# Cross-attention and a routed FFN: copies moved from VectorE to ScalarE and GpSimd, paddings written earlier, equal weight rows copied on the chip

## What is computed

```python
# x, ctx: (64, 128, 512) float32; mask: (64, 128)
x = x + xattn(layernorm(x), ctx, mask)      # softmax(x ctx^T / sqrt(512)) ctx, one head, per batch entry
x = x + ffn(layernorm(x))                   # 8192 tokens, 8 experts, top 2 of 8

scores = softmax(h @ G)                     # G: (512, 8); h is the normalised token
w = top-2 of scores, zero elsewhere
out = sum_e w_e * (silu(h gate_e^T) * (h up_e^T)) down_e^T     # expert width 64
out = out + sum_e w_e * (h A_e^T) B_e^T                        # rank 16
```

## Time and profile before

| | before |
| --- | --- |
| median of 3 runs | 509.11 us (508.49 to 510.6) |
| the profiled execution | 508.56 us, its span 506.8 us |
| busy, share of the span | PE 97%, PEld 86%, DVE 92%, ACT 68%, POOL 57% |
| bytes | HBM read 114.04 MB, written 78.73 MB; 373 GB/s by the DMA engines |
| granted PE clock | 0.99 in the mean, 1.00 during the sweep |

### The profile page before, as it was taken

The page is one execution under the profiler, slowest core; times in us unless marked ns, Lnnn a source line. Parts: engine busy times, 40 slices in busy tenths (PEclk is TensorE's granted clock), DMA queues, the critical chain, the costliest instruction groups (busy, mean ns, idle before and its releaser), DMA issues.

```text
span 506.8 us, 16153 instructions
## 1 busy us (share of the span) xinstructions
PE 489.3 (97%) x4040; PEld 434.1 (86%) x4040; DVE 464.8 (92%) x1855; ACT 343.3 (68%) x927; POOL 290.4 (57%) x411
## 2 busy tenths in 40 slices
PE   7999999999999999899999999999999999999994
PEld 7888888888888887789888999988999999999992
DVE  5899999999999998789989999998999999999995
ACT  4777888878877788778767887876444444444441
POOL 4227677667777568866775445444445445445444
PEclk9999999999999999999999999999999999999997
DMA  8999999999999999999999999969999999999941
GB/s 303 400 317 343 405 408 405 404 397 408 406 408 402 404 327 308 381 383 412 412 413 412 409 403 375 364 243 327 418 414 415 415 417 416 416 414 415 370 170 69
DMA packets 65607, 189.10 MB, mean 373 GB/s; under 512 B 9582, under 2 KB 9710, under 8 KB 65520
## 3 DMA queue, kind: packets, MB, share of 16 engines
q1 hardware_dynamic: 44352, 120.20, 62.2%
q0 software_dynamic: 20800, 67.65, 33.5%
q10 hardware_dynamic: 368, 0.22, 0.1%
HBM read 114.04 MB, written 78.73 MB: 380 GB/s over the span
## 4 chain that ended last, share of the span: by engine, by line
PE 48%; DVE 5%; POOL 5%; issue 5%; ACT 1%; POOLq 0%; ACTq 0%; DVEq 0%
PE rd L519 11%; PE bank L519 11%; PE bank L497 10%; PE rd L535 6%; PE rd L536 5%; PE rd L526 3%; POOL z_rows L1252 2%; DVE z_own L1140 1%; DVE z_shared L1140 1%; DVE ggT_b L1130 1%; POOL x_rows L1240 1%; PE bank L370 1%; DVE ggT_a L1129 1%; DVE xe L797 1%; DVE t L1113 1%
## 5 line engine op out<-in xcount | busy, mean ns | idle before, releaser
L674 ACT COPY hT<-bank 128x512 f32<-128x512 f32 x140 | 82.0, 586 | 50.6 <-PE bank L497 49.8
L1240 POOL DMA_INDIRECT x_rows<-xe x64 | 64.5, 1008 | 43.9 <-DVE xe L797 26.4
L519 PE MATMUL bank<-wg_sb,hT 128*128 x560 | 80.3, 286 | 0.4 <-ACT hT L674 0.4
L519 PE MATMUL rd<-wg_sb,hT 128*128 x560 | 80.2, 286 | 0.0
L370 PE MATMUL bank<-cc_sb,xnT 128*128 128x136 f32 x512 | 80.1, 286 | 0.0
L519 PEld LDWEIGHTS bank<-wg_sb,hT 128*128 128x128 f32 x560 | 72.6, 190 | 0.6 <-issue 0.6
L519 PEld LDWEIGHTS rd<-wg_sb,hT 128*128 128x128 f32 x560 | 72.6, 190 | 0.1
L370 PEld LDWEIGHTS bank<-cc_sb,xnT 128*128 128x128 f32 x512 | 68.4, 191 | 0.3
L535 PE MATMUL rd<-dn_a,ggT_a 128*128 x140 | 67.1, 480 | 1.4 <-DVE ggT_b L1130 1.3
L1255 POOL DMA_INDIRECT out_x<-z_shared x41 | 39.9, 973 | 42.8 <-DVE z_shared L1140 38.7
L1140 DVE SCALAR_TENSOR_TENSOR z_shared<-rd,z_shared 128x512 f32<-128x512 f32 x77 | 57.7, 749 | 2.1 <-PE rd L536 0.4
(11 more groups left out here) (185 smaller groups left out, 1183.1 us busy)
## 6 DMA issues: line engine op xcount, KB each, us to landing
cc_sb<-in_cc SPq DMA_DIRECT2D x64, 532.0 KB, 7.3
z_shared<-z_rows SPq DMA_DIRECT2D x41, 516.0 KB, 20.2
x_sb<-in_x SPq DMA_DIRECT2D x64, 256.0 KB, 6.4
z_own<-z_rows SPq DMA_DIRECT2D x29, 516.0 KB, 19.0
z_shared<-x_rows SPq DMA_DIRECT2D x36, 260.0 KB, 12.0
z_own<-x_rows SPq DMA_DIRECT2D x34, 260.0 KB, 11.1
z_rows<-pad SPq DMA_DIRECT2D x8, 516.0 KB, 7.6
wg_sb<-in_wg SPq DMA_DIRECT2D x8, 288.0 KB, 6.0
```

The source lines that it names most:

```text
L519: mm = pe.matmul(gu_ps[q % 2][:, 0:GU], hT[:, q % 2, k, :], wg_flat[:, bass.ds(at + k * GU, GU)], start=(k == 0), stop=(k == KD - 1))
L674: act.copy(hT[:, q % 2, :, :], hT_ps[q % 2][:].rearrange("p (k s) -> p k s", k=KD)).then_inc(hT_ready, 1)
L1240: pool.indirect_dma_start(out=x1_rows[:, :], out_offset=rows_at(row, ROW1), in_=row, in_offset=None, bounds_check=ROWS - 1, oob_is_err=Fal ...
```

## The change

DVE's `keep_part` becomes an ACT copy with a scale, called between `keep_pT` and `keep_prod`; DVE's `mask_scores` waits for it. `number` moves from DVE (after the fourth tile's sum of weights) to POOL, behind the scatter of the same step. The eight paddings of `x1_rows` go from tiles 10, 16, ... 52 to tiles 6, 7, 8, 8, 9, 9, 10 and 11. Of an odd down piece only the rows from `KG` are loaded (64 KB); its high part is taken of these rows alone, `dn_hi` is zero in the others (a memset on POOL), and instead of `down_left` ACT copies the equal rows of the even piece, as POOL has left them.

```diff
+PADDED_AT = [6, 7, 8, 8, 9, 9, 10, 11]
...
+        def down_rows(i):
+            return slice(0, P) if i % 2 == 0 else slice(KG, P)
...
-                if n % 6 == 4 and (n - 10) // 6 in range(E):
-                    at = (PADS + [NOWHERE])[(n - 10) // 6]
-                    if n == 10:
-                        sp.wait_ge(pad_set, 2)
-                    sp.dma_start(x1_rows[at:at + P, :], pad[:, D:ZW]).then_inc(padded[0], 16)
+                for i in range(E):
+                    if n == PADDED_AT[i]:
+                        at = (PADS + [NOWHERE])[i]
+                        if i == 0:
+                            sp.wait_ge(pad_set, 2)
+                        sp.dma_start(x1_rows[at:at + P, :], pad[:, D:ZW]).then_inc(padded[0], 16)
                 if n + 6 in SUMS_AT:
                     i = SUMS_AT.index(n + 6)
-                    sp.dma_start(dn_part(i).bitcast(F32), dn[:, i % 2, i // 2, :]).then_inc(dn_loaded, 16)
+                    if i % 2 == 0:
+                        sp.dma_start(dn_part(i).bitcast(F32), dn[:, i // 2, :]).then_inc(dn_loaded, 16)
+                    else:
+                        sp.dma_start(dn_part(i)[KG:P, :].bitcast(F32), dn_rest[:, i // 2, :]).then_inc(dn_loaded, 16)
...
-                act.activation(dn_hi[:, i % 2, :].bitcast(F32R), dn_part(i).bitcast(F32), ACT.Copy, scale=const_sb[:, SIGN:SIGN + 1]).then_inc(dn_hi_ready, 1)
+                if i == 1:
+                    act.wait_ge(dn_hi_set, 1)
+                own = down_rows(i)
+                act.activation(dn_hi[own, i % 2, :].bitcast(F32R), dn_part(i)[own, :].bitcast(F32), ACT.Copy, scale=const_sb[own, SIGN:SIGN + 1]).then_inc(dn_hi_ready, 1)
+
+            def down_same(i):
+
+                act.wait_ge(dn_ready, i)
+                act.copy(dn_part(i)[0:KG, :], dn_part(i - 1)[0:KG, :].bitcast(F32)).then_inc(dn_low_left, 1)
...
+            def keep_part(n):
+
+                m, b = divmod(n, TB)
+                act.wait_ge(scores_done, n + 1)
+                act.activation(x_sb[:, n % RX, D:D + E], sc_ps[:, S:S + E], ACT.Copy, scale=std1[:, m % 2, b:b + 1]).then_inc(part_ready, 1)
...
                 if in_sweep(t, 2):
                     keep_pT(t - 2)
+                if in_sweep(t, 1):
+                    keep_part(t - 1)
                 if in_sweep(t, 2) and t % 2 == 0:
                     keep_prod((t - 2) // 2)
                 if t + 2 in SUMS_AT:
                     down_hi(SUMS_AT.index(t + 2))
                 if t in SUMS_AT:
-                    down_left(SUMS_AT.index(t))
+                    i = SUMS_AT.index(t)
+                    if i % 2 == 0:
+                        down_left(i)
+                    else:
+                        down_same(i)
                 if in_sweep(t, 0):
                     keep_xT(t)
...
             def mask_scores(n):
                 dve.wait_ge(scores_done, n + 1)
+                dve.wait_ge(part_ready, n + 1)
...
-                dve.tensor_scalar(x_sb[:, n % RX, D:D + E], sc_ps[:, S:S + E], std1[:, m % 2, b:b + 1], None, ALU.mult).then_inc(part_ready, 1)
...
-                dve.tensor_scalar(xe[:, slots_of(m), TOKEN].bitcast(I32), const_sb[:, IDS:IDS + TB], float(TB * P * m), None, ALU.add).then_inc(token_ready, 1)
...
+                pool.tensor_scalar(xe[:, own, TOKEN].bitcast(I32), const_sb[:, IDS:IDS + TB], float(TB * P * m), None, ALU.add).then_inc(token_ready, 1)
...
                 pool.wait_ge(dn_low_left, i + 1)
+                pool.wait_ge(dn_hi_ready, i + 1)
                 pool.tensor_tensor(dn_part(i), dn_part(i).bitcast(F32), dn_hi[:, i % 2, :], ALU.add).then_inc(dn_ready, 1)
...
+            pool.memset(dn_hi[:, 1, :], 0.0).then_inc(dn_hi_set, 1)
             pool.wait_ge(pad_set, 1)
             pool.wait_ge(const_loaded, 16)
...
                     scatter_x1(t - 10)
+                if in_sweep(t, 9) and (t - 9) % TB == 0:
+                    number((t - 9) // TB)
```

More of the change, by code:

```diff
@@ L78 @@
 assert len(SUMS_AT) == 2 * E
+PADDED_AT = [6, 7, 8, 8, 9, 9, 10, 11]
+assert len(PADDED_AT) == E
 TICKS = 2 * NQ + 3
@@ L93, with xattn_moe @@
 NCONST = PACK + len(GROUPS)
-def xattn_moe(nc, x, cc, mask, wg, dn, g, consts, out):
+def xattn_moe(nc, x, cc, mask, wg, dn, dn_rest, g, consts, out):
     with ExitStack() as stack:
@@ L201, in xattn_moe @@
             sem, ("strips_done", "strips_ready", "prod_done", "prod_ready", "part_ready"))
-        after_set = sem("after_set")
+        after_set, dn_hi_set = sem("after_set"), sem("dn_hi_set")
         top_ready, which_ready, pair_ready, gap_step, turn_step, lexp_ready, hot_ready = map(
@@ L776, in mask_scores @@
                                          rowmin[:, n % 2, :]).then_inc(masked_ready, 1)
-            def keep_part(n):
-                m, b = divmod(n, TB)
-                dve.tensor_scalar(x_sb[:, n % RX, D:D + E], sc_ps[:, S:S + E], std1[:, m % 2, b:b + 1], None, ALU.mult).then_inc(part_ready, 1)
             def row_weights(n):
@@ L872, in weigh_row @@
                                          op0=ALU.mult, op1=ALU.mult).then_inc(weight_ready, 1)
-            def number(m):
-                dve.tensor_scalar(xe[:, slots_of(m), TOKEN].bitcast(I32), const_sb[:, IDS:IDS + TB], float(TB * P * m), None, ALU.add).then_inc(token_ready, 1)
             def centre_g():
@@ L1005, in _ @@
                     mask_scores(t - 1)
-                    keep_part(t - 1)
                 j = t // TB if t % TB == 2 and t // TB in range(1, NB) else None
@@ L1025, in _ @@
                     weigh_inverse((t - 9) // TB)
-                    number((t - 9) // TB)
                 if in_sweep(t, 3) and j is None:
@@ L1157, in _ @@
                     weigh_sum(NB - 1)
-                    number(NB - 1)
                     weigh_inverse(NB - 1)
@@ L1211, in norms, with number @@
                 pool.tensor_tensor(xe[:, own, SHIFT], neg[:, 1, :], xe[:, own, RSTD], ALU.mult).then_inc(norm_step, 1)
+            def number(m):
+                own = slice(TB * m % RE, TB * m % RE + TB)
+                pool.tensor_scalar(xe[:, own, TOKEN].bitcast(I32), const_sb[:, IDS:IDS + TB], float(TB * P * m), None, ALU.add).then_inc(token_ready, 1)
             def gaps(m):
@@ L1364, in _ @@
             norms(NB - 1)
+            number(NB - 1)
             gaps(NB - 1)
@@ L1419 @@
     down, lora_b = down.transpose(2, 0, 1), lora_b.transpose(2, 0, 1)
-    back = np.stack([np.concatenate([down[:Q], lora_b, lora_b, down[Q:], again], 0) for again in (down[:Q], down[Q:])], 1)
+    back = np.concatenate([down[:Q], lora_b, lora_b, down[Q:], down[:Q]], 0)
     consts = np.zeros((P, NCONST), np.float32)
@@ L1440 @@
         consts[j * GP:j * GP + E, at:at + E] = np.eye(E)
-    arrays = {"x": x, "cc": cc, "mask": mask, "wg": into, "dn": back, "g": g, "consts": consts}
+    arrays = {"x": x, "cc": cc, "mask": mask, "wg": into, "dn": back, "dn_rest": down[Q:], "g": g, "consts": consts}
     arrays = {f"in_{n}": np.ascontiguousarray(a) for n, a in arrays.items()}
```

## The result

| | before | after |
| --- | --- | --- |
| median | 509.30 us (508.37 to 511.02, 22 runs) | 512.28 us (509.79 to 516.02, 22 runs) |
| ratio | | 1.0056, 95% interval 1.0044 to 1.0068 |
| the profiled execution | 508.56 us, span 506.76 | 512.79 us, span 510.74 |
| bytes | HBM read 114.04 MB | HBM read 112.46 MB |

A forecast was written before the change was run, and what follows sets the result against it. DVE was taken to lead most of the sweep and PE the second phase. The profiled 508.56 us - 4.7 (sweep) + 3.15 (copies' waits) = 507.0, or 507.6 as median, with an eight-in-ten range of 504.2 to 511.0.

The forecast's parts named there:

- the sweep's gain: Sweep over 64 tiles: lighter DVE work saves 3.7 us in tiles 9 to 49 and 1.0 after, 4.7 in all.
- the forecast wait: Step 59: ACT's copy of piece 13 waits for POOL's piece 12, delaying PE by 2.6 us.
- PE becomes the bound: Mid-sweep: DVE's four tiles fall below PE's, so only 0.26 of the 0.64 us saved counts, with the hiccups.
- Its pace, 11.9: PE's own time for four tiles, from an early group of 11.83 us plus half a rank.
- the fourth rival: Sweep: PE's pace is 12.1 us, not 11.9, so the gain is 2 us: 510.3 us; chance 0.10.
- DVE at 11.52: Sweep: DVE's four tiles shrink by 0.64 us to 11.52 without keep_part and number.
- the second rival: Sweep: ACT's keep_part copy comes late, DVE's add_readout reaches PE late, the gain is gone: 512.3 us; chance 0.11.
- no gain is counted: Early paddings and lighter loads: 391 GB/s later in the sweep, but no DVE instruction waits for loads, so 0.
- the loads as a rival: Early paddings delay a load of x, or 32-row loads hold the rings, 1 to 3 us: 509.6 us; chance 0.09.
- The waits of the copies: Sweep's end: ACT's copies wait for POOL at steps 59 and 63; 2.6 - 0.65 + 1.3 - 0.1 = 3.15 us lost.
- the signs named for being wrong: Sweep's end: ACT waits below 1 us at steps 59 and 63, or a sweep ending before 206 us, would refute it.
- The second phase, 0 within 0.3: From the first block's matmul to the end: paced by PE, unchanged, 0 within 0.3 us.

The follow-up runs named there:

- f2: The changed kernel with the last down pieces at other steps, each copy at least three steps after its source: 505.82 us, ratio 0.9942 to the kernel before.
- g3: The changed kernel with the later copies and keep_part moved back to DVE: 508.61 us, ratio 0.9977 to the kernel before.
- f1: The changed kernel without the copies, every down piece loaded whole as before; moves and early paddings stay: 507.33 us, ratio 0.9956 to the kernel before.
- g4: The changed kernel with later copies, leaving out one of four slices of the scores' contraction on PE: 503.20 us, ratio 0.9868 to the kernel before.
- i1: The kernel before with the early paddings alone: ratio 0.9999 to the kernel before, in a session at 509 us.
- g1: The kernel before with keep_part on ACT and number on POOL alone, paddings and loads as before: ratio 1.0007 to the kernel before.
- i2: The kernel before with keep_part on ACT and number on POOL alone, run again in another session: ratio 1.0003 to the kernel before.
- f3: The kernel before with the copies of the odd down pieces alone: 514.84 us, ratio 1.0115 to the kernel before.
- f4: The changed kernel with 40 constant matmuls ahead of TensorE's wait at step 59: 511.25 us, ratio 1.0043 to the kernel before.
- e1: The changed kernel without the copies, in a session where the kernel before took 526.7 us: 528.29 us, ratio 1.0030 to the kernel before.

## Why the prediction was wrong, point by point

Two of its steps failed: the sweep's gain, which came out at 2.1 us instead of 4.7 because PE's and DVE's paces were both taken too low, and a term that the sum didn't have, the clock after the forecast wait, 1.3 us. Of the 2.6 us of missing gain 1.8 lie in tiles 9 to 49, where PE leads, 0.6 in tiles 49 to 57, where DVE leads, and 0.2 ahead of tile 9.

**PE becomes the bound: right. Its pace, 11.9: wrong.** The chain shows it (f2), and g3 that `keep_part` did it. But four tiles take 12.08 in the mean in after and 12.04 in f1, not 11.9. By the first matmul of each tile, six of f1's ten groups from tile 9 to 49 have steps of 2.74, 3.36, 2.73 and 3.14, 11.97 in all, and the others take up to 12.39; in after and f2 every second group has 2.91 or 2.92 instead of 2.74, which f1 hardly has, so it comes with the edit of the odd pieces, about 0.1 in four tiles (which instruction makes it I didn't trace). I took the pace from one early group of the earlier trace rows and added half a `rank` by guess. It is the fourth rival's case: its 12.1 and its gain of 2 us are what the sweep shows, 1.9 in tiles 9 to 49 for my 3.7.

**DVE at 11.52: wrong, 11.83.** That is the mean of g4, where DVE leads. I subtracted the 0.64 from 12.16, a group of four tiles without a hiccup, while before takes 12.27 in the mean; g4's two shortest groups take 11.66. The other 0.14 is mostly the mask, which in g4 starts 137 ns after the MAX8 ahead of it where it took 107 in before (means of tiles 13 to 45). With `keep_part` back on DVE (g3) it is 107 again, so the move itself costs this. ACT's copy took 267 ns and not my 0.17 us, and DVE waited for it 2.7 us in all. That is the second rival's mechanism, in a size that cost next to nothing. Between tiles 49 and 57, where DVE leads in both kernels (20.64 of 21 us busy, 20.70 in the earlier trace rows), 0.36 came instead of 1.0.

**The paddings, "no gain is counted": the total right, the reason wrong.** They gain nothing alone (i1), but without them `keep_part`'s move gains nothing either (g1, i2). I had the number: 4.93 MB in four tiles. At the 406 GB/s of the earlier trace rows that is 12.1 us, the kernel's pace, so an estimate from my own rows put the loads level with PE, behind DVE. Without the paddings four tiles move 4.75 MB, 11.7 us, and PE is next. The estimate falls short of the size: with the moves alone four tiles took 12.32 (g1) and 12.34 (i2). I compared 391 GB/s with 406 as if it were slack to spare, and named the loads as a rival only for the early stretch. The Trainium skill, "DMA: Bandwidth & Descriptors", section "Where 436 GB/s comes from", gives 435 GB/s as the ceiling of the ports, and about 358 as the limit of the HBM side, which it says binds between HBM and SBUF. By the first, as an estimate from the page's figure, four tiles would need 11.3 us and the loads would not have led; by the second 13.8, more than any run took. No stretch of 50 us or more read here moved over 408 GB/s (g1, 51 to 101 us), 6% below the first and 14% above the second, and the measured figure decides.

**The waits of the copies: right, in mechanism and size.** Forecast for tile 59: 2.6 us; 2.45 came. Given back after it: 0.65; 0.49 came at tile 61. At tile 63: 1.3; 1.36 came. Into the second phase: -0.1; -0.09. f1, f2 and f3 show that the wait for POOL is the cause. Neither of the signs named for being wrong appeared: ACT waited 3.0 and 1.9 us, and the sweep ended after 206.

**A term was missing: the clock, 1.3 us.** I priced the wait by its length alone. The Trainium skill, "TensorE: Matmul & The Clock Gate", section "HAM oscillation — how this bites in real kernels", tells of a kernel whose matmuls run at the half clock after TensorE has waited for data. The traces agree: 0.50 after the wait at step 59 in after and f3, and 1.00 in f4, where TensorE worked through it. A wait of 2.6 us stood in my sum, and what it would do to the clock was not asked. Summed, the last stretch lost 4.8 us (lead of 2.10 at tile 57, -2.68 at block 0) where 3.15 were forecast.

**The second phase, 0 within 0.3.** In the profiled executions it took 298.25 us, 1.30 more than before. But with the same second phase it took 297.98 in f1, 296.86 in f2, 297.38 in g3, 297.86 in i2, 298.37 in f3 and 297.24 in g1, and in f4, the changed kernel but for its 40 matmuls, 297.25. That is a scatter of single executions of 1.5 us, and before's 296.95 was at its lower end; the profiled executions differ by 4.2 where the medians differ by 3.0, as before's lies 0.7 below its median and after's 0.5 above. I had given such scatter nothing.

**The sum.** 507.0 was forecast for the profiled execution and 512.8 came: 2.6 of gain that wasn't there, 1.3 of clock, 0.3 in small delays between tiles 57 and 63, 1.3 of the second phase's scatter, and 0.25 more outside the span. The first two decided: with the waits as forecast and the gain at its real 2.1 the change costs 1 us, and the clock makes that 2.4. The measured 512.3 is also the second rival's number, 512.3, but by chance: that rival had the sweep gain nothing, at 12.2 us or more for four tiles, and it gained.

**Open.** What holds TensorE up at 527 us, what makes the longer steps of after and f2, and whether the loads' bytes or their order let the paddings matter. The changed kernel itself was not run at 527 us. Whether the 32-row loads cost more than their bytes is open too: in after they took 5.2 us from issue to landing, and the 256 KB of an even piece 5.5, in the same queue.

## What to carry to other kernels

Before an engine is relieved, work out the pace of every other resource in the same unit, the bytes of a period over the highest rate that the profile shows among them: the gain goes only as far as the nearest of them, and two edits that are each worth nothing can be worth something together. When a copy on the chip takes the place of a load, it inherits the time at which its source is finished; put it as many steps behind its source as the source's own chain is long (here three steps instead of one turned 512.3 into 505.8 us). A wait of TensorE is to be priced with the clock that is granted after it: here the longer wait cost half as much again, the shorter one nothing more.

## What the runs showed of the hardware

**The clock.** TensorE's stand of 2.3 us in after (2.65 in f3) was followed by some 3.4 us at 0.50 and a loss of 1.3 us (1.1 in f3). The second wait, 1.21 us without a matmul in after, was followed by no fall. With TensorE kept at work through the first (f4) there was none either.

**The same program can be 3.4 to 3.8% slower, and in another way.** The kernel before took 509.2 to 509.3 us in the result and in three sessions, and 526.7 and 528.7 in two others. At 527 us TensorE is late once in four tiles. e1, timeline (start, us, instruction, idle time before):

```profile
98.39 0.64 PE L387 MATMUL rd<-cc_sb,g_strip 128*32 128x128 f32 x16
...
100.49 0.27 ACT L594 COPY g_parts<-rd 128x128 f32<-128x128 f32 x1 [0.86 <-PE rd L387]
...
100.80 0.28 PE L394 MATMUL rd<-const_sb,g_parts 128*128 128x16 f32 x1 [0.51 <-ACT g_parts L594]
```

and the waits of 36 to 184 us:

```profile
PEld rd L394 <- ACT g_parts L594: 7.1, 10, 0.8
ACT g_parts L594 <- PE rd L387: 6.5, 8, 0.9
```

By the records the strips' matmuls end at 99.03, yet ACT, idle since 99.63, gets their result at 100.49, 1.4 us later. The records' ends are modelled, so either the real end or the word of it was late; the trace doesn't tell which. f1, the same kernel at 509 us, has no wait for L387's result in its list. The second phase's start is the other part: from the first matmul of block 0 to that of block 20 it takes 51.8 us in e1 and 40.7 in f1. In that stretch the granted clock is 0.50 for 6.9 us in e1 (222.2 to 229.1) and 1.00 throughout in f1, which is at most 3.5 of the 11 us. What holds TensorE up there no run shows; a gain of half a per cent found in one condition needn't be there in the other.

**A small copy out of PSUM on ACT isn't small.** 128x8 with a scale took 267 ns, more than the 173 of the 128x16 copy without one.
